# Alignment paths to experts: tests and row normalisation on another engine, statistics by quarters, part of the logits behind the first expert

## The chip, the cores and the metric

The kernel runs on one core of a Trainium2 chip. Its engines are TensorE (PE, with its weight load PEld), VectorE (DVE), ScalarE (ACT), GpSimd (POOL) and SyncE (SP), which issues the DMAs. Each has its own instruction stream, and they wait for one another by semaphores. The metric is the device time of one execution in microseconds. PE's granted clock is given as a share of 2.4 GHz: 1.00 is 2.4 GHz and 0.50 is 1.2 GHz.

## The reference

32 sequences of 128 tokens with 128 features, f32. Four blocks follow one another, each added to x with a tanh gate:

```python
x = x + tanh(g_xattn[0]) * mlstm_attention(layernorm(x), ctx, ctx, ...)
x = x + tanh(g_ffn[0])   * quantised_ffn(layernorm(x), W1, b1, W2, b2)
x = x + tanh(g_xattn[1]) * aligned(ctx, layernorm(x))
x = x + tanh(g_ffn[1])   * experts(layernorm(x), gate_weight, w1, b1, w2, b2)

def align_one(small, large):                # 128 tokens each
    R = dtw_cost(pairwise_euclidean(small, large))
    i_idx, j_idx, valid = backtrack(R)       # the cheapest monotone path
    return zeros.at[j_idx].add(small[i_idx] * valid)

def experts(x, ...):                         # 8 experts, hidden size 512
    logits = einsum('bld,ed->ble', x, gate_weight)
    kth_val = sort(logits.reshape(-1))[4 * 128 * 6 - 1]
    gates = logits * (logits >= kth_val)
    h = gelu(einsum('bld,ehd->bleh', x, w1) + b1)
    y = einsum('bleh,edh->blde', h, w2) + b2.T
    return einsum('blde,ble->bld', y, gates)
```

The part in question lies between the third block's backtracking and the fourth block's first experts.

## The kernel before

The residual `xs` stays in SBUF, tokens on partitions, 32 sequences side by side; they are worked in eight groups of four (`G4` = 8), a group being a tile of 128x512. The order on each engine is written out by hand, and every hand-over is a semaphore that counts up.

Backtracking leaves for each row of the path where it enters and leaves it. From these DVE makes a centre `ec` and a half width `eT[:, 1]` for each sequence (up to line 1106). Then, by groups:

- ACT makes the distances `pathm[:, b] = |iota2 + ec|`, 128x128 for each sequence (line 621, semaphore `far_ready`).
- DVE compares them with the half width and so writes the 0/1 matrix of the path, `path` (`path_of`, a `tensor_scalar` through the helper at line 676, `path_ready`).
- PE multiplies it with the context, `bank(1 + g % 2)` (line 1501, `expanded`).
- DVE adds the product to `xs` (`add_expanded`, line 1116) and takes `bn_stats` of each sequence (`stats`, line 1122).
- Layer norm goes by halves of 16 sequences: `ln_stats` makes mean and variance in seven small operations (lines 682 to 688), ACT takes the root (line 426), `ln_scales` the reciprocal (line 700), and `ln_apply` normalises 16 sequences, one instruction each, into `x4` (line 676 again, `ln_done`). Groups 0 to 3 are normalised when DVE has all but the last group's sum; then come the last add, its statistics, and the second half.
- PE transposes a group (line 1510, banks 6 and 7) and, one group behind, makes its logits in f32 with `x4f` as weights and eight columns as moving data (line 1516, bank 3). ACT copies the transposed bank twice: f32 into one of two slots of `x4f` (line 631) and bf16 into `x4h` (line 632). POOL subtracts: `x4l = x4f - x4h` (line 397).
- After the last logits PE waits for all of `x4l` and starts the experts.

For each block of 512 tokens (8) and each expert (8) PE makes the hidden part with three bf16 products for each of four banks (`hidden`, lines 1525 to 1527), ACT applies GELU (line 639), POOL in blocks 0 and 1 and DVE later split off the low half, and PE makes the outputs from 48 small products (`outputs`, lines 1541 to 1543). `outputs` of an expert follows `hidden` of the next. Blocks 0 and 1 are computed before the gates are known: meanwhile DVE looks for the threshold in 17 rounds, each of which compares all logits with candidates and lets PE sum the counts over partitions with a product with ones (`counts`, line 1549, put into `hidden` of expert n for round n; PE waits there for `count_ready`). In block 2 the gates' products with the bias go between the experts in nine steps (`gated_bias`, lines 1555 and 1559): step e transposes gates of group e - 1 and multiplies those of group e - 2, with an ACT copy between them and one behind. From line 1190 on DVE makes the low halves and the gated sums.

Of the kernel before, what the change touches and what calls it, by code (L numbers as in the profile page):

```python
# [15 lines left out]
P = 128  # L16
B = 32
# [38 lines left out]
def program(nc, x, ctx_, g_x, g_f, if_w, if_b, on_w, a_w1, a_b1, a_w2, a_b2, gate_w, m_w1, m_b1, m_w2, m_b2, out):  # L56
    with ExitStack() as stack:
# [3 lines left out]
        def sem(name):  # L61
# [64 lines left out]
        x4f = A[:, 8192:9216].rearrange("p (s t) -> p s t", s=2)  # L126
# [95 lines left out]
            "x4_turned", "x4_kept", "x4_split", "logits_done", "count_ready", "count_all", "gates_ready", "late_added", "bias_added", "gb_kept",  # L222
# [87 lines left out]
        def _(pool):  # L310
# [83 lines left out]
            for g in range(G4):  # L394
                pool.wait_ge(S["x4_kept"], g + 1)
                w = slice(512 * g, 512 * g + 512)
                pool.tensor_tensor(x4l[:, w], x4f[:, g % 2, :], x4h[:, w], ALU.subtract).then_inc(S["x4_split"], 1)  # L397
# [12 lines left out]
        def _(act):  # L410
# [208 lines left out]
            for g in range(G4):  # L619
# [3 lines left out]
            ln(3, (0,))  # L623
            for g in range(G4):
                if g == 3:
                    ln(3, (1,))
# [25 lines left out]
            for e in range(1, E + 2):  # L652
                if e < E:
                    gelu(NS, e)
                if e - 1 < G4:
                    act.wait_ge(S["gt_turned"], e)
                    act.activation(gtT[:, (e - 1) % 2, :], PS[0:32, 6, 0:P], ACT.Copy).then_inc(S["gt_kept"], 1)
                if e >= 2:
                    act.wait_ge(S["gb_done"], e - 1)
                    act.activation(gbias[:, 512 * (e - 2):512 * (e - 1)], bank(7), ACT.Copy).then_inc(S["gb_kept"], 1)  # L660
# [6 lines left out]
        def _(dve):  # L667
# [10 lines left out]
            def ln_stats(n, h):  # L678
                w = slice(16 * h, 16 * h + 16)
# [428 lines left out]
            def path_of(g):  # L1108
                dve.wait_ge(S["far_ready"], g + 1)
                for b in range(4 * g, 4 * g + 4):  # L1110
                    ins = ts(path[:, b, :], pathm[:, b, :], eT[:, 1, b:b + 1], None, ALU.is_le)
                ins.then_inc(S["path_ready"], 1)

# [31 lines left out]
            link(dve.tensor_copy(lgf, bank(3, 0, B * E)))  # L1145
# [104 lines left out]
        def _(pe):  # L1250
# [244 lines left out]
            for g in range(G4):  # L1495
# [6 lines left out]
                ins.then_inc(S["expanded"], 1)  # L1502
            pe.wait_ge(S["w_split"], 2 * E)
            for g in range(G4 + 1):
                if g < G4:
# [110 lines left out]
```

## Time and profile before

| | us |
|---|---|
| median of 3 runs (lowest, highest) | 780.08 (777.25, 780.39) |
| the profiled execution's own time | 777.89 |
| its span | 776.2 |
| busy: PE / DVE / ACT / POOL | 597.0 / 582.3 / 399.8 / 125.9 |
| mean granted clock of PE | 0.881 |
| first distances on ACT | 374.67 |
| first transpose of x4's second half | 406.40 |
| first product of the experts | 418.32 |
| first output product of the experts | 425.49 |

Times of the trace count from the start of the span. A row of the timeline or of a group gives an instruction's full duration, which can overlap its successor's; the chain of waits gives only what each piece adds to it. An L and a number is a line of the kernel; line 676 is a helper for every `tensor_scalar` of DVE, so those are told apart by their tiles.

### The profile page before, as it was taken

The page shows a single profiled execution, that of the slowest core. Times are in us where ns is not written, and L with a number is a line of the kernel's source. Part 1 is how long each engine was busy: PE and PEld are TensorE (multiplying, and loading weights), DVE is VectorE, ACT ScalarE, POOL GpSimd, SP SyncE. Part 2 cuts the span into 40 slices and gives each one's busy share as a digit, 9 for nine tenths or more (in the row PEclk, how much of TensorE's full clock was granted, in tenths as well). Part 3 has the DMA queues.
Part 4 walks back from the last instruction along what each step waited for, and adds up shares of the span by engine and source line. Part 5 has one row for each costly group of instructions (what it writes and reads, how often), then busy time and mean ns, then how long its engine had stood idle before and what let it go on. Part 6 is the DMA issues. An engine that isn't in the chain of part 4 may idle for free.

```text
span 776.2 us, 17215 instructions
## 1 busy us (share of the span) xinstructions
PE 597.0 (77%) x6431; PEld 430.5 (55%) x6499; DVE 582.3 (75%) x1736; ACT 399.8 (52%) x719; POOL 125.9 (16%) x158
## 2 busy tenths in 40 slices
PE   3975899843505870038469999999999999999997
PEld 3973344321204570027357777766577777777776
DVE  6657688898978819999794565566587788887775
ACT  1434778677826342238425556555444544554552
POOL 3000044434000000000025777700000000000000
PEclk9999999975557795559766999999999999999999
DMA  8000000000001000005000000000000000010000
GB/s 227 29 0 1 3 2 4 2 1 0 0 0 55 1 3 0 1 14 149 1 0 1 2 2 1 2 2 1 1 16 2 15 0 14 0 41 0 14 2 14
DMA packets 19548, 12.09 MB, mean 16 GB/s; under 512 B 1085, under 2 KB 18329, under 8 KB 19481
## 3 DMA queue, kind: packets, MB, share of 16 engines
q1 hardware_dynamic: 19480, 11.22, 5.3%
q8 instruction: 40, 0.66, 0.3%
q14 instruction: 28, 0.22, 0.1%
HBM read 9.12 MB, written 2.10 MB: 14 GB/s over the span
## 4 chain that ended last, share of the span: by engine, by line
PE 64%; DVE 28%; ACT 3%; issue 3%; SPq 1%; DMA 0%; another core or an unknown queue 0%; DVEq 0%
PE PS L1526 8%; PE PS L1541 7%; PE PS L1543 7%; PE PS L1542 7%; PE PS L1527 7%; PE PS L1525 5%; DVE A L1094 3%; PE PS L1274 3%; DVE Bm L1065 3%; PE PS L1348 3%; DVE hmm L986 2%; DVE hmm L987 2%; DVE Bm L676 2%; PE PS L1358 2%; PE PS L1454 1%
## 5 line engine op out<-in xcount | busy, mean ns | idle before, releaser
L639 ACT ACTIVATE A<-PS,small_t 128x512 f32<-128x512 f32 x256 | 168.3, 687 | 124.0 <-PE PS L1527 122.4
L1541 PE MATMUL PS<-kT_w,A 128*128 128x128 bf16 x1024 | 174.8, 219 | 0.0
L1543 PE MATMUL PS<-kT_w,A 128*128 128x128 bf16 x1024 | 174.8, 219 | 0.0
L1542 PE MATMUL PS<-kT_w,A 128*128 128x128 bf16 x1024 | 174.8, 219 | 0.0
L1190 DVE TENSOR_TENSOR A<-A 128x512 bf16<-128x512 f32 x192 | 123.6, 688 | 11.9 <-ACT A L639 10.5
L1541 PEld LDWEIGHTS PS<-kT_w,A 128*128 128x128 bf16 x1024 | 100.2, 98 | 11.3 <-issue 4.6
L1542 PEld LDWEIGHTS PS<-kT_w,A 128*128 128x128 bf16 x1024 | 100.2, 98 | 6.6
L1526 PE MATMUL PS<-A,xn_w 128*128 128x512 bf16 (+1 forms) x256 | 98.1, 383 | 3.6 <-issue 0.4
L1543 PEld LDWEIGHTS PS<-kT_w,A 128*128 128x128 bf16 x1024 | 100.2, 98 | 0.0
L1527 PE MATMUL PS<-A,xn_w 128*128 128x512 bf16 (+1 forms) x256 | 98.3, 384 | 0.0
L1198 DVE SCALAR_TENSOR_TENSOR xs<-PS,A,xs 128x128 f32 (+1 forms) x192 | 54.1, 344 | 55.9 <-PE PS L1543 55.9
L1525 PE MATMUL PS<-A,xn_w 128*128 128x512 bf16 (+1 forms) x193 | 74.2, 385 | 0.0
L401 POOL TENSOR_TENSOR A<-A 128x512 bf16<-128x512 f32 x64 | 64.5, 1041 | 22.4 <-ACT A L639 22.4
L1527 PEld LDWEIGHTS PS<-A,xn_w 128*128 128x128 bf16 x256 | 25.2, 99 | 31.1 <-issue 1.6
L1462 PE MATMUL PS<-identf,Bm 64*64 64x64 f32 x2 | 0.6, 298 | 51.7 <-DVE Bm L1065 51.7
L1525 PEld LDWEIGHTS PS<-A,xn_w 128*128 128x128 bf16 x256 | 26.9, 105 | 22.2 <-issue 1.9
L1526 PEld LDWEIGHTS PS<-A,xn_w 128*128 128x128 bf16 x256 | 25.3, 99 | 21.6 <-issue 1.4
L397 POOL TENSOR_TENSOR A<-A 128x512 bf16<-128x512 f32 x8 | 9.4, 1184 | 158.8 <-ACT A L632 158.8
L1462 PEld LDWEIGHTS PS<-identf,Bm 64*64 64x64 f32 x2 | 0.3, 127 | 52.0 <-issue 49.2
L1348 PE MATMUL PS<-A,kT_w 32*128 32x256 f32 x256 | 25.2, 435 | 3.8 <-DVE A L862 3.8
L643 ACT ACTIVATE Bm<-PS 128x512 f32 x16 | 9.6, 597 | 33.3 <-PE PS L1543 33.3
L862 DVE TENSOR_TENSOR A<-Bm,PS 128x512 f32<-128x512 f32 x32 | 20.6, 684 | 7.5 <-ACT Bm L473 4.8
(317 smaller groups left out, 1203.8 us busy)
## 6 DMA issues: line engine op xcount, KB each, us to landing
slab<-in_L_ffn_w_dram SPq DMA_DIRECT2D x16, 256.0 KB, 3.0
xs<-in_x_dram SPq DMA_DIRECT2D x4, 512.0 KB, 5.7
cs<-in_ctx_dram SPq DMA_DIRECT2D x4, 512.0 KB, 6.5
out_dram<-xs SPq DMA_DIRECT2D x8, 256.0 KB, 2.5
xn_w<-in_L_ffn_W_dram SPq DMA_DIRECT2D x2, 256.0 KB, 2.8
onw_b<-n_L_xattn_outnorm_w_dram SPq DMA_DIRECT2D x1, 64.0 KB
ab_b<-in_L_ffn_b_dram SPq DMA_DIRECT2D x1, 64.0 KB
b2blk<-in_L_ffn_b_dram SPq DMA_DIRECT2D x4, 4.0 KB
```

The source lines that it names most:

```text
L401: pool.tensor_tensor(hl[:, e % 2, c, :], hf[:, e % 2, c, :], hh[:, e % 2, c, :], ALU.subtract).then_inc(S["h_low_pool"], 1)
L639: act.activation(hf[:, e % 2, c, :], bank(c), ACT.Gelu_apprx_tanh, bias=b1).then_inc(S["h_gelu"], 1)
L1065: dve.tensor_tensor_scan(rt[:, s + 1, 1:RTW], mins[:, s], dd[:, s], rt[:, s + 1, 0:1], ALU.min, ALU.add).then_inc(S["row_done"], 1)
L1190: dve.tensor_tensor(hl[:, e % 2, c, :], hf[:, e % 2, c, :], hh[:, e % 2, c, :], ALU.subtract).then_inc(S["h_low_dve"], 1)
L1198: ins = dve.scalar_tensor_tensor(out=row, in0=bank(4 + e % 2, P * k, P * k + P), scalar=gate, in1=row, op0=ALU.mult, op1=ALU.add)
L1348: ins = pe.matmul(PS[:, 2 + r, 0:256], kT[rows, P * b:P * b + P], qTm[rows, :, P * b:P * b + P], start=True, stop=True)
L1525: pe.matmul(bank(c), w1h[:, e, c, :], x4h[:, xw], start=True, stop=False)
L1526: pe.matmul(bank(c), w1h[:, e, c, :], x4l[:, xw], start=False, stop=False)
L1527: pe.matmul(bank(c), w1l[:, e, c, :], x4h[:, xw], start=False, stop=True).then_inc(S["h_ready"], 1)
L1541: pe.matmul(o, hh[:, e % 2, c, t], w2h[:, e, c, :], start=(c == 0 and k == 0), stop=False, skip_group_check=True)
L1542: pe.matmul(o, hh[:, e % 2, c, t], w2l[:, e, c, :], start=False, stop=False, skip_group_check=True)
L1543: ins = pe.matmul(o, hl[:, e % 2, c, t], w2h[:, e, c, :], start=False, stop=(c == NC - 1), skip_group_check=True)
```

## The change

- `path_of` moves from DVE to POOL, for all eight groups.
- The normalisation of groups 0 to 5 moves from DVE to POOL (`x4_apply`, semaphore `x4_early`); groups 6 and 7 stay on DVE (`x4_late`). POOL's order is: tests 0 to 4, rows 0 and 1, tests 5 and 6, rows 2 and 3, test 7, rows 4 and 5.
- Statistics become variances by quarters of eight sequences (four calls of `ln_stats` with `each=8`), with a root on ACT (`x4_root`) and a reciprocal on DVE (`x4_scale`, `x4_scales`) for each.
- `x4l` is made by DVE from the transposed bank in PSUM (`x4_low`) in place of POOL from `x4f`. The bank is free for the transpose two groups later only after it. `x4f` becomes eight slots in another place, the copy order on ACT is turned (bf16 first), and the logits go to bank 5.
- PE's order: expansions 0 to 3; then transposes in pairs with expansions 4 to 7 and logits 0 to 3 between them; transposes 6 and 7; hidden products of the first expert; logits 4 to 7; the other experts. The first expert waits for one `x4l` and the last sum alone.
- Round n of the count is summed in `hidden` of expert n + 1, and the nine steps of the gated bias begin at expert 2 of block 2, not at expert 1; three of them then have no `hidden` of block 2 beside them, where it was two.

```diff
@@ gpsimd
-            for g in range(G4):
-                pool.wait_ge(S["x4_kept"], g + 1)
-                w = slice(512 * g, 512 * g + 512)
-                pool.tensor_tensor(x4l[:, w], x4f[:, g % 2, :], x4h[:, w], ALU.subtract).then_inc(S["x4_split"], 1)
+            def path_of(g):
+                pool.wait_ge(S["far_ready"], g + 1)
+                for b in range(4 * g, 4 * g + 4):
+                    ins = pool.tensor_scalar(path[:, b, :], pathm[:, b, :], eT[:, 1, b:b + 1], None, ALU.is_le)
+                ins.then_inc(S["path_ready"], 1)
+            def x4_apply(g):
+                pool.wait_ge(S["x4_scales"], g // 2 + 1)
+                for b in range(4 * g, 4 * g + 4):
+                    ins = pool.tensor_scalar(x4[:, b, :], xs[:, b, :], lnt[:, 3, b:b + 1], lnt[:, 7, b:b + 1], ALU.subtract, ALU.mult)
+                ins.then_inc(S["x4_early"], 1)
+            for g in range(5):
+                path_of(g)
+            for g in range(2):
+                x4_apply(g)
+            for g in range(5, 7):
+                path_of(g)
+            for g in range(2, 4):
+                x4_apply(g)
+            path_of(G4 - 1)
+            for g in range(4, 6):
+                x4_apply(g)
@@ scalar
+            def x4_root(j):
+                w = slice(8 * j, 8 * j + 8)
+                act.wait_ge(S["bn_done"], 7 + j)
+                act.activation(lnt[:, 5, w], lnt[:, 4, w], ACT.Sqrt, bias=cst[:, 0:1]).then_inc(S["ln_sqrt"], 1)
+            def x4_keep(g):
                 act.wait_ge(S["x4_turned"], g + 1)
-                if g >= 2:
-                    act.wait_ge(S["logits_done"], g - 1)
-                    act.wait_ge(S["x4_split"], g - 1)
-                act.activation(x4f[:, g % 2, :], bank(6 + g % 2), ACT.Copy)
                 act.activation(x4h[:, 512 * g:512 * g + 512], bank(6 + g % 2), ACT.Copy).then_inc(S["x4_kept"], 1)
+                act.activation(x4f[:, g], bank(6 + g % 2), ACT.Copy).then_inc(S["x4_kept"], 1)
+            for g in range(6):
+                far(g)
+            x4_root(0)
+            for g in range(6, G4):
+                far(g)
+            for j in range(4):
+                if j >= 1:
+                    x4_root(j)
+                x4_keep(2 * j)
+                x4_keep(2 * j + 1)
@@ vector
+            def x4_scale(j):
+                dve.wait_ge(S["ln_sqrt"], 7 + j)
+                dve.reciprocal(lnt[:, 7, 8 * j:8 * j + 8], lnt[:, 5, 8 * j:8 * j + 8]).then_inc(S["x4_scales"], 1)
+            def x4_low(g):
+                w = slice(512 * g, 512 * g + 512)
+                dve.wait_ge(S["x4_kept"], 2 * g + 2)
+                dve.tensor_tensor(x4l[:, w], bank(6 + g % 2), x4h[:, w], ALU.subtract).then_inc(S["x4_split"], 1)
             for g in range(G4):
-                path_of(g)
-                if g >= 1:
-                    add_expanded(g - 1)
-                if g >= 2:
-                    ins = stats(g - 2)
-                if g == 5:
-                    link(ins)
-                    ln_stats(3, 0)
-                if g == 6:
-                    ln_scales(3, 0)
-            ln_apply(0, xs, x4)
-            add_expanded(7)
-            stats(6)
-            link(stats(7))
-            ln_stats(3, 1)
-            ln_scales(3, 1)
-            ln_apply(1, xs, x4)
+                add_expanded(g)
+                if g % 2 == 0 and g >= 2:
+                    x4_scale(g // 2 - 1)
+                ins = stats(g)
+                if g % 2:
+                    link(ins)
+                    ln_stats(3, g // 2, 8)
+                if g in (4, 6):
+                    for k in (g - 4, g - 3):
+                        x4_low(k)
+            x4_scale(3)
+            for g in range(G4 - 2, G4):
+                (four rows of tensor_scalar into x4, then x4_late)
+            for g in range(4, G4):
+                x4_low(g)
@@ tensor
+            def turn_x4(g):
+                (waits for x4_early or x4_late)
+                if g >= 2:
+                    pe.wait_ge(S["x4_kept"], 2 * g - 2)
+                    pe.wait_ge(S["x4_split"], g - 1)
+                (four transposes into bank 6 + g % 2)
+            for g in range(4):
+                expand(g)
+            for j in range(3):
+                turn_x4(2 * j)
+                turn_x4(2 * j + 1)
+                if j < 2:
+                    expand(2 * j + 4)
+                    expand(2 * j + 5)
+                if j >= 1:
+                    logits(2 * j - 2)
+                    logits(2 * j - 1)
+            turn_x4(6)
+            turn_x4(7)
+            pe.wait_ge(S["expanded_added"], G4)
+            pe.wait_ge(S["x4_split"], 1)
...
-                    if isinstance(blk, int) and blk * E + e < ROUNDS and c == (1 if blk or e else 2):
-                        counts(blk * E + e)
+                    if isinstance(blk, int) and 1 <= blk * E + e <= ROUNDS and c == 1:
+                        counts(blk * E + e - 1)
...
             hidden(0, 0)
+            for g in range(4, G4):
+                logits(g)
+            pe.wait_ge(S["x4_split"], G4)
...
-            for e in range(1, E + 2):
+            for e in range(1, E + 3):
                 if e < E:
                     hidden(NS, e)
-                if e == 1:
+                if e == 2:
                     pe.wait_ge(S["gates_ready"], 1)
                     pe.wait_ge(S["b2_in"], 64)
-                gated_bias(e)
+                if e >= 2:
+                    gated_bias(e - 1)
```

## Rows read from the trace of the kernel before

**Rows 1.** The page's slices of the span, 19.4 us each: busy tenths of TensorE and of VectorE

```profile
PE   3975899843505870038469999999999999999997
DVE  6657688898978819999794565566587788887775
```

**Rows 2.** The chain of waits, 374 to 407 us: start us, us, what

```profile
374.67 1.28 ACT Bm L621 x4
...
379.77 0.78 DVE Bm L676 x4
380.55 0.66 DVE xs L1116
381.21 0.78 DVE bns L1122 x4
...
388.66 0.19 DVE lnt L682
...
389.57 0.17 DVE lnt L688
...
394.47 5.92 DVE A L676 x16
...
406.40 1.12 PE PS L1510 x4
```

**Rows 3.** Windows by stage: us, busy of PE, PEld, DVE, ACT, POOL, clock, DMA, GB/s

```profile
374.67:394.40 19.73, 11.46 (x62) 10.22 (x63) 16.95 (x72) 9.76 (x33) 0.00 (x0) 0.76 0.00 1
394.40:406.40 12.00, 7.47 (x45) 6.54 (x44) 11.45 (x39) 4.43 (x9) 4.69 (x4) 0.64 0.00 1
406.40:418.32 11.92, 11.69 (x56) 11.65 (x58) 4.13 (x13) 4.34 (x8) 4.74 (x4) 0.50 0.00 1
418.32:425.49 7.17, 6.74 (x27) 2.94 (x27) 4.06 (x22) 5.30 (x8) 3.97 (x4) 0.83 0.00 0
```

**Rows 4.** Groups, 374 to 421 us: busy us, mean ns | idle us before, releaser

```profile
L621 ACT ACTIVATE Bm<-iota,ec 128x128 f32<-128x128 f32 x32 | 9.5, 389 | 8.3 <-DVE ec L676 8.3
...
L632 ACT ACTIVATE A<-PS 128x512 bf16<-128x512 f32 x8 | 4.8, 594 | 0.0
...
L676 DVE TENSOR_SCALAR Bm<-Bm,eT 128x128 f32<-128x128 f32 x32 | 6.9, 280 | 1.7 <-ACT Bm L621 1.6
```

**Rows 5.** Timeline of TensorE: start us, us, what, count, idle before and releaser

```profile
387.25 1.16 PE L1501 MATMUL PS<-cs,Bm 128*128 128x128 f32 x8 [1.05 <-DVE Bm L676]
...
390.59 2.07 PE L1501 MATMUL PS<-cs,Bm 128*128 128x128 f32 x8 [2.18 <-DVE Bm L676]
...
397.90 0.97 PEld L1516 LDWEIGHTS PS<-small_t,A 128*128 128x128 f32 x8 [0.76 <-ACT A L632]
...
406.40 1.12 PE L1510 MATMUL PS<-identf,A 128*128 128x128 f32 x4 [3.32 <-DVE A L676]
...
407.31 1.72 PE L1516 MATMUL PS<-small_t,A 128*128 128x8 f32 x8
```

**Rows 6.** Groups of GpSimd, whole span; the last line is line 397's own view

```profile
L338 POOL TENSOR_SCALAR identn<-identb 128x128 bf16<-128x128 bf16 x1 | 0.3, 297 | 0.1
...
L372 POOL TENSOR_TENSOR A<-Bm,onw_b 128x128 f32<-128x128 f32 x4 | 1.7, 453 | 0.1
...
L397 POOL TENSOR_TENSOR A<-A x8: 1151/1154/1282, 397.9 to 416.1; 128x512 bf16<-128x512 f32 x8
```

**Rows 7.** The timeline, TensorE's second count among the experts

```profile
423.96 0.39 PE L1549 MATMUL PS<-sel,ones 128*128 128x3 f32 x2 [0.43 <-DVE A L1156]
```

**Rows 8.** The timeline, TensorE's last step of the gated bias

```profile
555.89 1.12 PE L1559 MATMUL PS<-b2blk,A 32*128 32x512 f32 x2 [0.69 <-ACT Bm L660]
```

**Rows 9.** Windows of two to six us

```profile
382.00:388.00 6.00, 3.07 (x22) 2.69 (x23) 6.00 (x25) 2.13 (x8) 0.00 (x0) 1.00 0.01 3
...
390.00:392.00 2.00, 1.41 (x6) 1.41 (x7) 2.00 (x9) 0.09 (x1) 0.00 (x0) 0.52 0.00 0
...
400.00:402.00 2.00, 1.79 (x11) 1.70 (x10) 2.00 (x8) 0.57 (x2) 1.47 (x2) 0.58 0.00 0
```

More of the change, by code:

```diff
@@ L125, in program @@
         x4l = A[:, 6144:8192].bitcast(BF16)
-        x4f = A[:, 8192:9216].rearrange("p (s t) -> p s t", s=2)
+        x4f = Bm[:, 8192:12288].rearrange("p (g t) -> p g t", g=G4)
         hf = A[:, 9216:13312].rearrange("p (s c t) -> p s c t", s=2, c=NC)
@@ L618, in _, with far @@
             act.wait_ge(S["e_kept"], 1)
-            for g in range(G4):
+            def far(g):
                 for b in range(4 * g, 4 * g + 4):
@@ L651, in _ @@
                 keep_y(blk, E - 1)
-            for e in range(1, E + 2):
+            for e in range(1, E + 3):
                 if e < E:
                     gelu(NS, e)
[L655 to L660, printed above, removed]
+                if 2 <= e < G4 + 2:
+                    act.wait_ge(S["gt_turned"], e - 1)
+                    act.activation(gtT[:, (e - 2) % 2, :], PS[0:32, 6, 0:P], ACT.Copy).then_inc(S["gt_kept"], 1)
+                if e >= 3:
+                    act.wait_ge(S["gb_done"], e - 2)
+                    act.activation(gbias[:, 512 * (e - 3):512 * (e - 2)], bank(7), ACT.Copy).then_inc(S["gb_kept"], 1)
             with act.Fori(NS + 1, G4) as blk:
@@ L676, in ts, with ln_stats @@
                 return dve.tensor_scalar(out, a, s1, s2, op0, op1)
-            def ln_stats(n, h):
-                w = slice(16 * h, 16 * h + 16)
+            def ln_stats(n, h, each=16):
+                w = slice(each * h, each * h + each)
                 t = lambda k: lnt[:, k, w]
@@ L1106, in _ @@
             ts(ec[:], ec[:], pm[:, 11:12], pm[:, 12:13], ALU.mult, ALU.add).then_inc(S["e_kept"], 1)
[L1108 to L1112, printed above, removed]
             def add_expanded(g):
@@ L1494, in _, with expand @@
             pe.matmul(PS[HALF:P, 3, 0:2 * B], flip, logs[:, :, 1], start=True, stop=True).then_inc(S["e_turned"], 1)
-            for g in range(G4):
+            def expand(g):
                 pe.wait_ge(S["path_ready"], g + 1)
@@ L1502, in _, with logits @@
                 ins.then_inc(S["expanded"], 1)
-            pe.wait_ge(S["w_split"], 2 * E)
-            for g in range(G4 + 1):
-                if g < G4:
-                    pe.wait_ge(S["ln_done"], 3 * G4 - 4 + g + 1)
-                    if g >= 2:
-                        pe.wait_ge(S["x4_kept"], g - 1)
-                    for k in range(4):
-                        ins = pe.transpose(bank(6 + g % 2, P * k, P * k + P), x4[:, 4 * g + k, :], identf[:])
-                    ins.then_inc(S["x4_turned"], 1)
-                if g >= 1:
-                    pe.wait_ge(S["x4_kept"], g)
-                    for k in range(4):
-                        b = 4 * (g - 1) + k
-                        ins = pe.matmul(bank(3, E * b, E * b + E), x4f[:, (g - 1) % 2, P * k:P * k + P], small_t[:, 84:92], start=True, stop=True)
-                    ins.then_inc(S["logits_done"], 1)
-            pe.wait_ge(S["x4_split"], G4)
+            def turn_x4(g):
+                if g < 6:
+                    pe.wait_ge(S["x4_early"], g + 1)
+                else:
+                    pe.wait_ge(S["x4_late"], g - 5)
+                if g >= 2:
+                    pe.wait_ge(S["x4_kept"], 2 * g - 2)
+                    pe.wait_ge(S["x4_split"], g - 1)
+                for k in range(4):
+                    ins = pe.transpose(bank(6 + g % 2, P * k, P * k + P), x4[:, 4 * g + k, :], identf[:])
+                ins.then_inc(S["x4_turned"], 1)
+            def logits(g):
+                pe.wait_ge(S["x4_kept"], 2 * g + 2)
+                for k in range(4):
+                    b = 4 * g + k
+                    ins = pe.matmul(bank(5, E * b, E * b + E), x4f[:, g, P * k:P * k + P], small_t[:, 84:92], start=True, stop=True)
+                ins.then_inc(S["logits_done"], 1)
+            pe.wait_ge(S["w_split"], 2 * E)
+            for g in range(4):
[13 more added lines that the diff above has]
+            pe.wait_ge(S["x4_split"], 1)
             def hidden(blk, e):
@@ L1567, in _ @@
                 outputs(blk, E - 1)
-            for e in range(1, E + 2):
+            for e in range(1, E + 3):
                 if e < E:
                     hidden(NS, e)
-                if e == 1:
+                if e == 2:
                     pe.wait_ge(S["gates_ready"], 1)
                     pe.wait_ge(S["b2_in"], 64)
-                gated_bias(e)
+                if e >= 2:
+                    gated_bias(e - 1)
                 if e < E:
```

12 lines of the change are left out of this document (6 added, 6 removed).

## The prediction

> **What bounds the kernel now.** I read the page first, then the chain of waits, then windows by stage, then groups of instructions. The page's slices show TensorE (PE) full from the twenty-second slice on, behind a stretch in which VectorE (DVE) is the full engine [rows 1]. The chain goes through DVE from 374.67 us, where ScalarE (ACT) begins the distances |2k - c|, to the last normalised quarter, and from 406.40 through PE alone [rows 2]. By windows: 374.67 to 406.40 is DVE's (16.95 of 19.73 us, then 11.45 of 12.00), 406.40 to 418.32 PE's (11.69 of 11.92) at a granted clock of 0.50, the 1.2 GHz level [rows 3]. From 418.32 the experts begin, PE-bound to the end, so what counts is when the first output product starts, 425.49 now: every microsecond of it is a microsecond of the end, except what the later part of the diff adds. GpSimd (POOL) does nothing from 374.67 to 394.40 [rows 3].
>
> **The pieces and their prices.** Rows of groups and of the timeline overlap their successors, so for runs of like instructions I use what each adds, start to start. By the chain [rows 2] four path tests cost 0.78 us on DVE, one add of the expanded group 0.66, four statistics 0.78, the small operations from statistics to variance 1.08 (388.66 to 389.74), a row of the normalisation 0.37 (5.92 for 16). There are thirty-two tests [rows 4] and as many statistics. ACT makes a group of distances in 1.16 (32 starts in 9.46) and copies a bank of 512 in 0.594, 0.50 from start to start [rows 4]. On PE an expansion of a group is 1.16 us at 2.4 GHz and 2.07 at 1.2 GHz, a group's transpose 1.12 at 1.2 GHz, the logits of a group 1.72 at 1.2 GHz and, by their weight loads, 0.97 at 2.4 GHz [rows 5]. Some 0.2 of each is the last product's way out (the chain has 1.51 for the logits of 1.72), which the next work on PE doesn't wait for and the consumer does.
>
> **Part 1: tests and rows on POOL.** 32 tests (6.2 us by start to start) and 24 of the 32 row normalisations (24 x 0.37 = 8.9 us) leave DVE: 15.1 us. In exchange DVE gets the eight low parts x4l, read straight from PSUM, where POOL read the f32 copy: 8 x 0.66 (the add, of the same width and also with one PSUM operand, is the nearest row) = 5.3. Four variances of quarters instead of two of halves add 2 x 1.08. DVE falls by 7.6 us. POOL's price per instruction is not in the trace: no POOL tensor_scalar with a column operand over 128 f32 stands there. Low bound: the two-operation form with constants on 128 bf16 took 0.297, with the next start 0.24 later; high bound: the two-input tensor_tensor of 128 f32, 0.453 [rows 6]; but column operands could be worse than either, so for the range I go up to 0.6, a third above the highest row. I take 0.28 for a test and 0.35 for a row, near the one-input row with something for the columns. The eight late rows stay on DVE.
>
> **Part 2: the chain in the new order.** Times with the PE clock between its levels: an expansion 1.40 (between 0.95 and 1.85 without the way out), a transpose 0.65 (0.45 to 0.85), logits 1.35; 0.1 to 0.3 for each hand-over.
> First distances 375.95; four tests on POOL, 377.1; expansion, 379.0; DVE adds and takes statistics of groups 0 and 1, then the variance, 382.95. ACT's root is hidden under the add of group 2; the reciprocal ends at 383.8. POOL normalises groups 0 and 1 (8 x 0.35): 386.8. Transpose 1, 387.6. Behind it on PE stands expansion 4: 389.0. DVE adds group 4, reciprocal 1: 390.2. POOL, groups 2 and 3: 393.2; transpose 3, 394.0; expansion 6, queued behind that transpose: 395.4. DVE: add 6, reciprocal 2, statistics 6, low parts 2 and 3, add 7, statistics 7, variance (0.66 + 0.22 + 0.78 + 1.32 + 0.66 + 0.78 + 1.08): 401.2. The last root waits on ACT behind the four copies of groups 4 and 5, which wait for POOL (396.7 to 399.5) and transpose 5: root 402.7, reciprocal 403.1. Eight late rows 2.96: 406.0. Then a wait that before doesn't have: a bank is free for transpose 6 only when DVE has made low part 4, which is queued behind the late rows: 406.7; transpose 6, low part 5, transpose 7: **408.2** for the first expert product, where 418.32 stands now: 10.1 us earlier.
>
> **Part 3: what is given back.** The logits of groups 4 to 7 aren't removed; they stand on PE between the first expert's hidden products and the next's. Four groups cost 3.9 us at 2.4 GHz, 6.9 at 1.2 GHz; 5.4 is taken. The shift of the counting by one expert takes away the 0.43 us for which PE waited for the second count [rows 7]: the first count now has a whole first product around it. The 7.17 us from first expert product to first output product become 7.17 - 0.43 + 5.4, and 0.5 (between 0 and 1.3) if the clock has fallen in the narrow logits and the next six products go at 1.2 GHz as the first six do now. That is 12.6: output products from 420.8 instead of 425.49, 4.7 us gained.
>
> **Part 4: the gated bias, one expert later.** Of its nine steps two now stand with no hidden product between them, afterwards three. A lone step goes at 1.12 + 0.69 = 1.81 us (PE waits for ACT's copy) [rows 8], of which 1.05 is PE work that is only moved: 0.8 lost. Nothing to 1.8 is possible. Gates come later by one expert in DVE's order too, but its next low parts are wanted only one hidden product later.
>
> **Sum.** -10.1 + 5.4 (12.6 against 7.17) + 0.8 = -3.9 us. ACT's table load of 1.28 us before the first GELU has the logits beside it now. The copies of x4f into eight slots instead of two remove waits and cost nothing: ACT is busy for 9.76 + 4.43 of 31.7 us here [rows 3]. SP's queue has no edit. The profiled execution took 777.89 us (span 776.2, 1.7 around it) and would be 774.0; the runs' median is 780.08 (777.25 to 780.39), 2.2 above the profiled one, and by that the same sum gives **776.2**.
>
> **A rule weighed.** The trace shows POOL at 1.28 us at most for the subtraction of 512 when DVE runs beside it and 1.15 at least [rows 6]: no lock is to be seen there. The Trainium skill (GPSIMD Engine Reference, 3. Performance versus the Vector engine) holds VectorE about twice as fast for elementwise work, though it lets one-input operations off (4.1 Engine selection). Twice DVE's own 0.195 and 0.37 on POOL would be 0.39 and 0.74, and the chain above then ends at 417.3 with a total of +5.2 us, 785.3. The one-input row at 0.24 us start to start speaks against it. I count this in the slow-POOL rival.
>
> **The clock, the uncertain middle.** The granted clock was 1.00 from 382 to 388 with PE busy half the time, fell about 390, in an idle stretch of 2.18 us [rows 5], and was 0.50 even for the full stretch of transposes and logits from 406.40; in the experts' first 7.17 us it averaged 0.83, so 2.4 us of them went at 1.2 GHz [rows 3]. From 400 to 402, in the narrow logits, it fell to 0.58 [rows 9]. So logits alone don't lift it, and gaps end it. The new order has POOL's pace in front of PE, and gaps of 2 to 3 us before transposes 0 and 6.
>
> **Rivals.**
> Warm PE: if the expansions, spread out through the stage, hold the clock at 1.00, the chain ends at 405.3, logits take 3.9 and the first six products save 1.3: 405.3 + 9.3 + 0.8 - 425.49 = -10.1, so 770.0. For it: 382 to 388. Against it: the fall at 390. Chance 0.2.
> Cold PE: 1.2 GHz throughout: chain 412.1, logits 6.9, next six products +1.3: +2.3, so 782.4. The pipeline then gives nothing, since PE's own stretch of 11.9 us is only moved. Chance 0.15.
> Slow POOL, the one that ends slower: 56 instructions in series before groups 4 and 5 are ready. At 0.6 us for each they alone are 33.6 us; the chain ends at 418.6, total +6.5: 786.6. It decides from 0.475 us per instruction on (chain end 412.1 = 425.49 - 13.4). For it: column operands and a comparison are forms that no row has. Against it: both one-input rows under 0.3. Chance 0.15.
> My forecast has 0.5, its own range 773 to 780.
>
> **Range and chances.** Between the warm and the cold case, and a little of the slow one: 770 to 783. The measurement can't tell less than about 0.5%, 3.9 us, from no change, and the forecast lies on that line: half of its 0.5 counts as faster. With the warm case: faster 0.46; same (the other half, most of the cold one): 0.38; slower 0.16.
>
> **What would show it.** In the profile after: the first expert product near 408 (405 to 412); POOL tests at 0.25 to 0.3 us start to start and rows at 0.3 to 0.4; 64 narrow logits products, half of them behind the first expert; first output product near 421; the wait of transpose 6 put down to DVE's low part; three lone bias steps at the end of block 2. The forecast is wrong if POOL's pace is over 0.47 us, if the granted clock is above 0.8 or at 0.5 in all of 377 to 408, or if the experts' own rhythm changes, for which I see no reason.

## The result and the profile after

The changed kernel is slower, by about 1%: 787.34 us in the median (785.8 to 788.22, 4 runs) against 780.24 (777.25 to 781.0, 4 runs) for the kernel before on the same chip, ratio 1.0096 (95% interval 1.0065 to 1.0127). The forecast was 776.2 within 770 to 783.

The page of the kernel after, against [rows 1] (busy by engine, then the slices):

```profile
PE 603.5 (77%) x6499; PEld 431.5 (55%) x6499; DVE 573.0 (73%) x1704; ACT 400.6 (51%) x721; POOL 154.2 (20%) x206
...
DVE  6657678898979719998543556676478788887775
...
POOL 3000045434000000000893777700000000000000
```

DVE is no longer the full engine ahead of the experts: in the three slices that hold this stretch (the 20th to the 22nd) it read 794 and now reads 543, and POOL, 025 before (its subtractions, then work for the first experts), reads 893. The two groups of POOL that the change made (busy us, mean ns | idle before, releaser; [rows 4] has the tests as DVE's):

```profile
L403 POOL TENSOR_SCALAR A<-xs,lnt 128x128 f32<-128x128 f32 x24 | 18.8, 795 | 1.6 <-DVE lnt L1151 1.6
L397 POOL TENSOR_SCALAR Bm<-Bm,eT 128x128 f32<-128x128 f32 x32 | 18.6, 601 | 126.3 <-ACT Bm L640 126.3
```

The chain of waits after, where [rows 2] had DVE from 374.67 to 406.40 (start us, us, what):

```profile
374.82 1.28 ACT Bm L640 x4
...
376.21 11.63 POOL Bm L397 x20
387.84 6.26 POOL A L403 x8
394.10 4.64 POOL Bm L397 x8
398.74 6.26 POOL A L403 x8
405.00 2.33 POOL Bm L397 x4
407.33 1.50 issue
408.89 0.07 POOL A L403
...
409.68 5.47 POOL A L403 x7
415.19 1.13 PE PS L1547 x4
416.34 0.60 ACT A L650
...
417.43 0.20 ACT lnt L646
...
417.89 2.14 DVE A L706 x8
420.03 0.61 DVE A L1156
...
420.78 1.94 PE PS L1547 x8
422.72 0.43 PE PS L1578
```

From 376.21 to 415.15 the chain is POOL's own row of instructions, with one gap, from 407.33 to 408.89, in which it waits for the third reciprocal (the group's idle 1.6 us behind DVE's L1151). Twenty tests take 11.63 us, 0.58 each; eight rows 6.26, 0.78 each. The end of the chain is as forecast: the last root behind ACT's copies, eight late rows on DVE, low part 4, transposes 6 and 7. The windows by stage, as [rows 3]:

```profile
374.82:394.40 19.58, 9.63 (x37) 8.09 (x38) 8.88 (x35) 10.84 (x35) 18.19 (x29) 0.59 0.00 1
394.40:406.40 12.00, 6.35 (x31) 5.76 (x30) 5.54 (x20) 2.55 (x6) 12.00 (x19) 0.64 0.00 0
406.40:422.72 16.32, 11.55 (x64) 10.88 (x64) 8.90 (x31) 4.26 (x10) 7.18 (x10) 0.60 0.00 1
422.72:432.90 10.18, 10.18 (x61) 6.40 (x60) 3.57 (x15) 6.89 (x11) 5.48 (x6) 0.89 0.00 0
```

DVE is busy for 8.88 of 19.58 us where it was full, POOL for 18.19 of 19.58 and 12.00 of 12.00. First expert product at 422.7 (418.3 before), first output product at 432.7 (425.5), and from there 351.3 us to the end of the span (350.7).

One caution for all profiles below. In the attention stage, which no kernel here edits, the same instructions started up to 3.5 us apart from profile to profile (the last scores at 160.3 us in one, 163.8 in another), so I compare stages from the first distances on, which the cores reach at 374.7 to 378.1:

| kernel | first distances to first expert product: forecast by prices / measured | first distances to end of span | ratio to before (95% interval) |
|---|---|---|---|
| before | - / 43.6 | 401.5 | 1 |
| after | 33.5 in the prediction / 47.9 | 409.3 | 1.0096 (1.0065 to 1.0127) |
| tests back on DVE | 46.1 / 45.9 | 406.3 | 1.0074 (1.0053 to 1.0096) |
| rows back on DVE | 39.6 / 38.9 | 399.7 | 0.9985 (0.9966 to 1.0003) |
| both on DVE | 40.4 / 40.1 | 401.4 | 1.0021 (1.0007 to 1.0034) |
| rows as wide products on POOL | 42.8 / 41.6 | 403.2 | 1.0018 (1.0001 to 1.0034) |
| as rows back on DVE, logits in front | 44.6 / 44.3 | 405.2 | 1.0048 (1.0032 to 1.0064) |
| rows on ACT, low parts on POOL | 33 / 34.0 | 395.7 | 0.9924 (0.9907 to 0.9942) |
| rows on ACT, low parts on DVE | 35.7 / 35.9 | 401.1 | 0.9982 (0.9968 to 0.9995) |
| rows on ACT, low parts on POOL, late rows on DVE | 33 / 33.7 | 396.1 | 0.9925 (0.9901 to 0.9949) |
| before, subtraction behind the rows | 41.3 / 41.3 | 398.8 | 0.9969 (0.9956 to 0.9981) |

The first column is good to some 0.3 us: a few records of PE are missing, the very first product of the experts among them in the kernel before and in the three runs with tests, rows or both back on DVE, and the chain has a product 0.2 us later than the timeline.

The second column has a spread of its own. Behind the last steps of the gated bias in block 2 TensorE's granted clock can fall to 0.50, for a length that differs from profile to profile, also where the instructions there are the same. Windows of 25 us around these steps (columns as in [rows 3]) of the kernel before, of "before, subtraction behind the rows" and of "logits in front":

```profile
550.00:575.00 25.00, 24.00 (x236) 15.91 (x239) 15.31 (x34) 11.03 (x19) 0.00 (x0) 0.93 0.04 12
550.00:575.00 25.00, 24.31 (x247) 16.16 (x247) 16.86 (x42) 12.30 (x21) 0.00 (x0) 1.00 0.04 12
552.00:577.00 25.00, 23.84 (x213) 14.53 (x211) 13.45 (x31) 10.57 (x18) 0.00 (x0) 0.86 0.04 12
```

From the first output product to the end of the span these three take 350.7, 348.9 and 352.8 us. So a difference of some 2 us in the second column, and 4 between the last two of these, can come from there; the ratios rest on the medians of all runs, and how often each length occurs in those is not known.

### The profile page after: what moved, and what is told of

Same layout as the page of the kernel before. It is cut to its first block, busy times and chain, and to the rows that moved or that the text cites. A ratio compares the mean times of both kernels' runs of the same rounds, so it can differ in the third digit from the quotient of the medians.

```text
span 784.1 us, 17295 instructions
## 1 busy us (share of the span) xinstructions
PE 603.5 (77%) x6499; PEld 431.5 (55%) x6499; DVE 573.0 (73%) x1704; ACT 400.6 (51%) x721; POOL 154.2 (20%) x206
## 4 chain that ended last, share of the span: by engine, by line
PE 64%; DVE 25%; POOL 5%; ACT 3%; issue 2%; SPq 1%; DMA 0%; DVEq 0%; POOLq 0%
PE PS L1594 7%; PE PS L1596 7%; PE PS L1595 7%; PE PS L1578 7%; PE PS L1579 7%; PE PS L1580 7%; DVE A L1124 3%; PE PS L1308 3%; PE PS L1382 3%; DVE Bm L1095 3%; POOL Bm L397 2%; POOL A L403 2%; DVE hmm L1016 2%; DVE hmm L1017 2%; PE PS L1392 2%
## 5 line engine op out<-in xcount | busy, mean ns | idle before, releaser
L1594 PE MATMUL PS<-kT_w,A 128*128 128x128 bf16 x1024 | 174.8, 219 | 0.0
L1594 PEld LDWEIGHTS PS<-kT_w,A 128*128 128x128 bf16 x1024 | 100.2, 98 | 10.6 <-issue 3.8
L1579 PE MATMUL PS<-A,xn_w 128*128 128x512 bf16 (+1 forms) x256 | 98.3, 384 | 0.0
L1578 PE MATMUL PS<-A,xn_w 128*128 128x512 bf16 (+1 forms) x256 | 98.1, 383 | 0.0
L1580 PE MATMUL PS<-A,xn_w 128*128 128x512 bf16 (+1 forms) x256 | 98.1, 383 | 0.0
L420 POOL TENSOR_TENSOR A<-A 128x512 bf16<-128x512 f32 x64 | 64.6, 1041 | 31.6 <-ACT A L669 31.6
L397 POOL TENSOR_SCALAR Bm<-Bm,eT 128x128 f32<-128x128 f32 x32 | 18.6, 601 | 126.3 <-ACT Bm L640 126.3
L1208 DVE TENSOR_SCALAR_CACHE_REDUCE sel<-PS 128x3 f32<-128x3 f32 (+1 forms) x16 | 2.6, 161 | 33.3 <-PE PS L1602 33.3
```

Of the source, the lines that this page charges most:

```text
L397: ins = pool.tensor_scalar(path[:, b, :], pathm[:, b, :], eT[:, 1, b:b + 1], None, ALU.is_le)
L420: pool.tensor_tensor(hl[:, e % 2, c, :], hf[:, e % 2, c, :], hh[:, e % 2, c, :], ALU.subtract).then_inc(S["h_low_pool"], 1)
L1578: pe.matmul(bank(c), w1h[:, e, c, :], x4h[:, xw], start=True, stop=False)
L1579: pe.matmul(bank(c), w1h[:, e, c, :], x4l[:, xw], start=False, stop=False)
L1580: pe.matmul(bank(c), w1l[:, e, c, :], x4h[:, xw], start=False, stop=True).then_inc(S["h_ready"], 1)
L1594: pe.matmul(o, hh[:, e % 2, c, t], w2h[:, e, c, :], start=(c == 0 and k == 0), stop=False, skip_group_check=True)
```

## The experiments

**What an instruction costs on POOL.** A kernel that only times instructions on loaded tiles (one execution).

```diff
+ for k in range(8):
+     pool.tensor_scalar(py[:, k, :], xs[:, k, :], 0.5, None, ALU.is_le)    # and: a column; mult; two operations
...
+ for k in range(4):
+     pool.tensor_tensor(four tiles of py, four of xs, four columns with a step of zero, ALU.subtract)
```

> This kernel computes nothing of the reference: it only times instructions of GpSimd and VectorE on loaded x, eight or sixteen of each form in a row. Three readings of GpSimd's 0.58 us for a path test and 0.78 us for a normalised row of 128 f32. (A) The operand that is a column of one value per partition costs: the forms with constants stay at 0.24 to 0.30 us start to start, with one column 0.58, with two 0.78, and a column form over 512 elements costs about 0.3 us more than one over 128, since the columns are paid once. (B) The comparison and the second operation cost, by element: constant forms are as slow as column forms, and 512 elements take nearly four times as long as 128. (C) VectorE, which worked beside it, slowed GpSimd: alone, all forms are at 0.30 or less. Second question: the rows of the normalisation on VectorE took 0.26 us alone but 1.25 us whenever GpSimd's 512-wide subtraction ran in the kernel before. If the two lock each other out, VectorE's 24 rows beside GpSimd's eight subtractions of 512 show some of 1.2 us and beside GpSimd's column rows some of 0.9 to 1.0 us; if it was chance, all are at 0.23 to 0.26 us. Statistics (bn_stats, one input) should show no such thing.

The timeline of POOL in that kernel: start us, us of the whole run, line, forms, count. Lines 51 to 66 are, in order: is_le with a constant, is_le with a column, mult with each, subtract and mult with constants, the same with columns; 69 and 72 the two column forms over 512; 75 a two-input subtraction of 512 whose second input is four columns, spread by a step of zero (78, not shown, multiplies in the same way); 83 a subtraction of two tiles of 512, and 88 and 103 rows with two columns, all three beside work of DVE.

```profile
10.69 3.98 POOL L51 TENSOR_SCALAR py<-xs 128x128 f32<-128x128 f32 x8 [10.27 <-DMA xs<-in_x_dram]
14.78 4.64 POOL L54 TENSOR_SCALAR py<-xs,col 128x128 f32<-128x128 f32 x8
19.50 3.99 POOL L57 TENSOR_SCALAR py<-xs 128x128 f32<-128x128 f32 x8
23.59 4.66 POOL L60 TENSOR_SCALAR py<-xs,col 128x128 f32<-128x128 f32 x8
28.34 4.91 POOL L63 TENSOR_SCALAR py<-xs 128x128 f32<-128x128 f32 x8
33.36 6.21 POOL L66 TENSOR_SCALAR py<-xs,col 128x128 f32<-128x128 f32 x8
39.67 6.17 POOL L69 TENSOR_SCALAR py<-xs,col 128x512 f32<-128x512 f32 x4
45.95 8.24 POOL L72 TENSOR_SCALAR py<-xs,col 128x512 f32<-128x512 f32 x4
54.27 4.03 POOL L75 TENSOR_TENSOR py<-xs,col 128x512 f32<-128x512 f32 x4
...
66.93 9.80 POOL L83 TENSOR_TENSOR py<-xs 128x512 f32<-128x512 f32 x8 [4.52 <-DVEq L123]
81.11 12.96 POOL L88 TENSOR_SCALAR py<-xs,col 128x128 f32<-128x128 f32 x16 [4.37 <-DVEq L128]
...
116.83 4.23 POOL L103 TENSOR_SCALAR py<-xs,col 128x128 f32<-128x128 f32 x4 [0.21 <-DVEq L143]
```

Start to start: 0.498 and 0.580 for one operation with a constant and a column, comparison and product alike; 0.614 and 0.776 for two operations. Over 512 elements 1.54 and 2.06. So neither reading (A) nor (B) holds whole: of 0.58 only 0.08 is the column, and of 0.78 0.16; a comparison costs no more than a product. Most of it goes by element: (1.54 - 0.58) / 384 is 2.5 ns, and 3.3 ns with two operations. (C) falls: alone they are as slow as in the kernel. The two-input tensor_tensor of 512 takes 1.01, less than two thirds of the tensor_scalar of 512 with one column. DVE's side of the same kernel:

```profile
62.60 4.19 DVE L121 TENSOR_SCALAR dy<-xs,col 128x128 f32<-128x128 f32 x16 [61.74 <-POOLq L80]
66.94 13.97 DVE L125 TENSOR_SCALAR dy<-xs,col 128x128 f32<-128x128 f32 x24
81.09 8.82 DVE L130 TENSOR_SCALAR dy<-xs,col 128x128 f32<-128x128 f32 x32 [0.18 <-DVE dy L125]
94.24 6.29 DVE L135 BATCH_NORM_STATS2 bst<-xs 128x6 f32<-128x128 f32 x32 [4.33 <-POOLq L90]
...
116.80 3.60 DVE L145 TENSOR_TENSOR dy<-xs 128x128 f32<-128x128 f32 x16 [3.22 <-POOLq L100]
```

Sixteen rows alone are 0.26 each. Beside POOL's subtractions eight were done in 9.76 us, 1.22 for each pair of one row and one subtraction. That is near the sum of 0.26 for a row and 1.01 for a two-input form of 512, as if each ran only while the other didn't; this is called the lock below. Beside POOL's column rows 32 take 8.82, 0.28 each, and statistics 0.20 as alone. Beside DVE's two-input additions POOL's rows rise from 0.78 to 1.06.

**Tests, rows, or both back on DVE.**

```diff
# tests (first run), rows (second), both (third): the same instructions, on DVE
-                    ins = pool.tensor_scalar(path[:, b, :], pathm[:, b, :], eT[:, 1, b:b + 1], None, ALU.is_le)
+                    ins = ts(path[:, b, :], pathm[:, b, :], eT[:, 1, b:b + 1], None, ALU.is_le)
...
-                    ins = pool.tensor_scalar(x4[:, b, :], xs[:, b, :], lnt[:, 3, b:b + 1], lnt[:, 7, b:b + 1], ALU.subtract, ALU.mult)
+                    ins = ts(x4[:, b, :], xs[:, b, :], lnt[:, 3, b:b + 1], lnt[:, 7, b:b + 1], ALU.subtract, ALU.mult)
```

> The changed kernel with the path tests back on VectorE; rows of groups 0 to 5 stay on GpSimd. Theory P (GpSimd's price per instruction, 0.58 and 0.78 us in series, is the whole loss, the new order costs next to nothing): GpSimd has 24 x 0.78 = 18.8 us left; but the rows of a pair can only start when its reciprocal is there, so the first expert product comes at about 420.9 instead of 422.7, and the time is about 785.5 us (ratio to before 1.007). Theory C (the new couplings are the loss: transposes wait for the low parts, expansions stand behind transposes, PE at 1.2 GHz in the gaps; GpSimd only fills waits): 787, no change.

> The changed kernel with the row normalisation of groups 0 to 5 back on VectorE (0.26 us a row), tests stay on GpSimd. Theory P: GpSimd 32 x 0.58 = 18.6 us from 376.2, it is through at 394.9; VectorE gets 24 x 0.26 = 6.2 us; first expert product at about 414.4, time about 779 us (ratio 0.998). Theory C: the order is the same, so at least 785 us.

> The changed kernel with tests and rows on VectorE, GpSimd does nothing in this stretch; pipeline, quarters, low parts on VectorE, logits behind the first expert and the later bias stay. Theory P: VectorE is the bound again (27 us of its own), first expert product at about 415.2, time about 779.8 us (ratio 1.000), so the pipeline without GpSimd is worth nothing, and nothing is lost. Theory C: at least 785 us, as the couplings are all there.

Measured: 785.43, 777.79 and 780.68 us, before 778.78; ratios in the table. Theory P hits all three within 2 us and each stage within 0.7 us (table). Theory C wanted 787 for the first, whose runs reach from 782.46 to 787.36, and 785 or more for the other two, none of whose runs exceeds 781.82: it falls by these two. The rows are what makes the change slow. With them back the pipeline is level with the kernel before (0.9985, its interval reaches 1.0003); with the tests back too it is 0.2% behind.

**Rows on POOL in the cheaper form.**

```diff
-                for b in range(4 * g, 4 * g + 4):
-                    ins = pool.tensor_scalar(x4[:, b, :], xs[:, b, :], lnt[:, 3, b:b + 1], lnt[:, 7, b:b + 1], ALU.subtract, ALU.mult)
+                link(pool.tensor_tensor(g4(x4, g), g4(xs, g), last(lnt[:, 3, 4 * g:4 * g + 4], P), ALU.subtract))
+                pool.tensor_tensor(g4(x4, g), g4(x4, g), last(lnt[:, 7, 4 * g:4 * g + 4], P), ALU.mult).then_inc(S["x4_early"], 1)
```

> The changed kernel with one edit: a group's rows on GpSimd as two tensor_tensor instructions of 512 with the columns spread by a step of zero, in place of four tensor_scalar of 128 with two columns. Alone the forms took 1.01 us for each 512 and 0.776 for each 128, so a group is 2.1 us instead of 3.1. Theory P (GpSimd's price in series is the loss): first expert product 42.8 us after the first distances (47.9 in the changed kernel), time about 782 us, ratio to before 1.004. If the price beside VectorE is not what it is alone, the group stays at 2.5 us or more and the time at 784 or more.

780.59 us, before 779.69, ratio 1.0018: of the 7 us lost most came back by one edit of POOL's instruction form. A subtraction and a product of 512, 1.04 us each, stand in the place of four rows, 3.1 us. The group of the subtractions:

```profile
L402 POOL TENSOR_TENSOR A<-xs,lnt 128x512 f32<-128x512 f32 x6 | 6.3, 1042 | 1.6 <-DVE lnt L1150 1.6
```

**The logits in front again.**

```diff
+            logits(4)
+            logits(5)
             turn_x4(6)
             turn_x4(7)
+            logits(6)
+            logits(7)
...
             hidden(0, 0)
-            for g in range(4, G4):
-                logits(g)
```

> The run with the rows on VectorE and the tests on GpSimd, with the logits of groups 4 to 7 put back ahead of the first expert (4 and 5 before the transposes of 6 and 7, 6 and 7 behind them). What is this part of the change worth? By the prices of the trace: the first expert product comes 5 us later, but then 3.3 us fewer stand before the first output product: 2 us slower than that run, so about 779.8 us, ratio 1.001. Rival: the logits only fill gaps in which PE waits for VectorE, so it is as fast as that run (777.8), and the split of the logits is worth nothing.

782.02 us, 4 us more than with the logits behind the first expert, where 2 were expected. The rival falls. The first expert product came 5.4 us later (5 expected), but the way from there to the first output product was only 1.4 us shorter (8.1 against 9.5) in place of 3.3: the expert's first products ran at 1.2 GHz for some 5.5 us (0.43 us each until 424.7, in the chain). Narrow logits had run right ahead of them; that these are the cause is what the trace suggests, not something that I isolated.

**Each piece where it is cheapest.**

```diff
# DVE: tests; a column -m*r after each reciprocal.  ACT: all rows
+                link(dve.reciprocal(lnt[:, 7, w], lnt[:, 5, w]))
+                dve.scalar_tensor_tensor(out=lnt[:, 6, w], in0=lnt[:, 3, w], scalar=-1.0, in1=lnt[:, 7, w], op0=ALU.mult, op1=ALU.mult)
...
+                    ins = act.activation(x4[:, b, :], xs[:, b, :], ACT.Identity, scale=lnt[:, 7, b:b + 1], bias=lnt[:, 6, b:b + 1])
# POOL: low parts (left out in the second version, where DVE keeps them)
+                pool.tensor_tensor(x4l[:, w], x4f[:, g, :], x4h[:, w], ALU.subtract).then_inc(S["x4_split"], 1)
# PE: expand(4), expand(5) ahead of turn_x4(0); no wait for x4_split where POOL has the low parts
```

> Each piece of the pipeline on the engine where its measured price is lowest: tests on VectorE (0.195 us), all 32 rows on ScalarE as x*r + (-m*r) with two columns (0.3 us each by its distances, which carry one column), low parts by GpSimd as one subtraction of 512 (1.0 to 1.2 us) from the eight slots of x4f, expansions 4 and 5 ahead of the first transposes. Theory P (only the price of column instructions on GpSimd made the change slower, the pipeline itself is sound): first expert product 33 us after the first distances (before 43.65, changed kernel 47.9), time about 771.7 us, ratio 0.991. Theory C (the finer order brings as many new waits as it removes): 777 or more. GpSimd's subtractions may lock VectorE's last tests and cost 1 to 2 us.

> As the run with the low parts on GpSimd, but these stay on VectorE from PSUM, and a transpose waits for them as in the changed kernel. Theory P: VectorE is the bound again with 27 us; first expert product 35.7 us after the first distances, time about 774.5 us, ratio 0.9945. Theory C: 778 or more.

The first is the fastest version: 773.14 us, 0.9924, where 771.7 and 0.991 were expected; theory C's 777 or more falls. The second comes at 777.28 us, 0.9982, where 774.5 and 0.9945 were expected: a miss, just under theory C's 778. The pieces of the first, busy us and mean ns:

```profile
L649 ACT ACTIVATE A<-xs,lnt 128x128 f32<-128x128 f32 x32 | 12.7, 492 | 0.0
...
L409 POOL TENSOR_TENSOR A<-Bm,A 128x512 bf16<-128x512 f32 x8 | 9.2, 1159 | 152.2 <-ACT Bm L644 152.1
...
L723 DVE TENSOR_SCALAR Bm<-Bm,eT 128x128 f32<-128x128 f32 x32 | 6.8, 279 | 1.9 <-ACT Bm L633 1.9
```

ACT is its bound now, at 3.07 us for eight rows in the chain (0.38 each; 0.3 was expected). The second has its first expert product where it was forecast, but 13.9 us pass from there to the first output product, where the first needs 10.3. The chains of both, second kernel first; L1594 and L1589 are the sixteen logits products of groups 4 to 7 (32 records):

```profile
415.93 4.30 PE PS L1594 x32
420.23 0.44 PE PS L1625
```

```profile
413.93 3.47 PE PS L1589 x32
417.40 0.23 PE PS L1620
```

In the second kernel the clock falls within the logits (0.78 over their 4.30 us) and the next expert's products take 0.43 in place of 0.22 us each. The 3.6 us between 13.9 and 10.3 are more than the 2.8 by which the second version misses its forecast. What decides between the two was not isolated. An edit on top of the first version:

```diff
-            x4_apply(6)          # ACT
-            x4_apply(7)
+            (eight rows of groups 6 and 7 by ts on DVE, behind x4_scale(3))
```

> The fastest version so far (tests on VectorE, rows on ScalarE, low parts on GpSimd) with the rows of groups 6 and 7 on VectorE, which is idle by then, since ScalarE now ends the stretch with 3.07 us for eight rows (0.38 each). VectorE's eight take 2.1 us, unless one of GpSimd's subtractions runs beside them: each would cost 0.9 more. Expected by the prices: first expert product 0.6 to 1.3 us earlier than in that version (34.0 us after the first distances there), time about 772.2 us, ratio 0.9915. Rival: the lock takes it back, no difference from 0.9924.

773.56 us, 0.9925: no difference. The lock was there. The timeline has two of GpSimd's subtractions beside the eight rows, which take 3.96 us in place of 2.1, the longest 1282 ns:

```profile
406.52 3.96 DVE L721 TENSOR_SCALAR A<-xs,lnt 128x128 f32<-128x128 f32 x8
...
407.08 2.30 POOL L409 TENSOR_TENSOR A<-Bm,A 128x512 bf16<-128x512 f32 x2 [2.92 <-ACT Bm L644]
```

But it is not what took the gain back. PE has the logits of groups 2 and 3 (3.21 us, at a granted clock of 0.50) ahead of transpose 6 in its order; they end at 410.24, and the transposes follow without a wait. So the rival's lock is seen and its number is right, but the wait that ends last is PE's own. In the profile the first expert product comes 0.3 us earlier than in the version without the edit and the first output product 1.2 us earlier (43.2 against 44.4 us after the first distances); the clock in block 2, low for longer there (0.86 over 25 us against 0.93), takes this back.

**The lock in the kernel before.**

```diff
             for g in range(G4):
+                pool.wait_ge(S["ln_done"], 3 * G4 + 4)
                 pool.wait_ge(S["x4_kept"], g + 1)
...
-                pool.tensor_tensor(x4l[:, w], x4f[:, g % 2, :], x4h[:, w], ALU.subtract).then_inc(S["x4_split"], 1)
+                pool.tensor_tensor(x4l[:, w], x4f[:, g, :], x4h[:, w], ALU.subtract).then_inc(S["x4_split"], 1)
```

> The kernel before with one edit: GpSimd's subtractions of 512 begin only when VectorE's last normalised row is done (x4f has eight slots for it). Theory L (the two engines lock each other out: VectorE's row takes 1.2 us beside a subtraction and 0.26 alone): all 32 rows at 0.26, the first transpose of the second half comes 2.7 us earlier, first expert product about 2.3 us earlier since GpSimd needs 9.2 us after the rows; time about 776.4 us, ratio 0.997. Theory N (no lock; the long rows have another cause): rows as before, and the first expert product some 3 us later, as GpSimd starts late: 782 us.

776.02 us, ratio 0.9969, as theory L has it. ACT's copies into eight slots also wait no longer for the logits and the subtraction of two groups before; this part of the edit is not separated from POOL's wait. The line's own view there (duration min/median/max, first and last start):

```profile
L674 DVE TENSOR_SCALAR A<-xs,lnt x32: 329/339/345, 395.2 to 407.2; 128x128 f32<-128x128 f32 x32
...
L398 POOL TENSOR_TENSOR A<-Bm,A x8: 1152/1154/1157, 407.6 to 415.4; 128x512 bf16<-128x512 f32 x8
```

No row is above 345 ns any more. The same view of the kernel before:

```profile
L676 DVE TENSOR_SCALAR A<-xs,lnt x32: 330/342/1262, 394.4 to 410.0; 128x128 f32<-128x128 f32 x32
```

There the longest took 1262 ns. So the lock is what made rows long, and theory N falls. How much the wait is worth is less clear than the hit on 776.4 suggests. The first expert product comes 2.3 us earlier after the first distances, as forecast. The first output product comes only 1.0 us earlier (49.8 against 50.8): all nine wide products before the first count go at 1.2 GHz in the chain (0.43 us each), where before the last two had 0.22. The other 1.8 us by which this profile's stretch to the end is shorter are in the clock, which didn't fall in block 2. That the profile ends as forecast is in part luck.

## Why the prediction was wrong

**POOL's price (part 1) is the step that failed.** It took 0.28 us for a test and 0.35 for a row; they are 0.58 and 0.78, 37.3 us for 56 instructions instead of 17.4. With these two numbers put into the prediction's own chain, and 0.26 for the late rows, its groups 2 and 3 are normalised at 404.7; as there, rows 4 and 5 can start 3.5 us later, behind expansion 6 and the third reciprocal, and take 6.2; the rest of its chain is 7.8 us. The first expert product then comes at about 422.2; it came at 422.7. So the slow-POOL rival, given 0.15, is what happened, and its turning point of 0.475 us per instruction was passed: the mean is 0.67 (37.3 / 56). Where exactly the turn lies no run shows. The bounds were wrong, too. [Rows 6] gave 0.297 from a bf16 tile with constants and called it the nearest row; in f32 two operations with constants take 0.61, so its closeness was in the name of the instruction and not in its data type (how much of the difference the data type makes was not timed). "Both one-input rows under 0.3" is this one row of [rows 6]. The trace of before did have GpSimd's tensor_scalar in f32 with two operations, unused by the prediction: line 357, seven times 128x32 at 216 ns, nearly three quarters of the bf16 row's 297 for a quarter of its elements. And the two-input 0.453 was taken as the dearest form, while at 512 elements the two-input form is the cheaper one (1.01 against 1.54 us). The widened end, 0.6, rested on no row, and the normalising rows lie beyond even that.

**The rule that was weighed.** Twice DVE's price, 0.39 and 0.74 with a total of 785.3, was set aside for the closeness of that one row. Measured, POOL's 0.58 and 0.78 are three times DVE's 0.195 and 0.26, and the runs' median is 787.34. The exemption of one-input operations, which the prediction named with it (Trainium skill, GPSIMD Engine Reference, 4.1 Engine selection), is what these rows contradict: even with one operation and a constant GpSimd's f32 instruction takes 0.498 us.

**The lock that was missed.** "No lock is to be seen there" was read from POOL's durations, 1.15 to 1.28 us; the one that waits is DVE. It stood in the trace of before. Windows of DVE's rows there, without and with a subtraction beside them:

```profile
394.39:396.00 1.61, 1.61 (x7) 0.50 0.00 0
...
397.93:400.40 2.47, 2.47 (x3) 0.99 0.00 0
```

Seven rows in 1.61 us (0.23 each), then three in 2.47 (0.82; subtractions are busy for 2.38 of the 2.47). The 0.37 us of the prediction was a mean of 0.26 and 1.2. The Trainium skill (SBUF — State Buffer, Who interferes with whom) says that a tensor_scalar of VectorE in a two-port mode and GpSimd hold a shared pair of ports in turn, each for a whole instruction; beside the subtractions the traces agree, with 1.22 us for a pair in the timing kernel; which mode VectorE was in, none of them shows. Beside POOL's tensor_scalar the measurement differs: VectorE's rows stay at 0.28. Had this been read, DVE's 8.9 us for 24 rows would have been 6.2, and the alternative, to move the subtraction and not the rows, would have been in sight. No run moves the subtraction alone; to delay it has the ratio 0.9969, and the best version, 0.9924, combines the tests and rows taken off POOL, the rows put on ACT and the subtraction kept on POOL.

**The other numbers.** From first expert to first output product: 12.6 forecast, 10.0 measured, as the clock held its 2.4 GHz through the logits (3.47 us for four groups) and nothing was lost in the next expert; with the low parts on DVE and the rows on ACT it is 13.9. The gated bias: 0.8 forecast, 0.6 as the longer way from the first output product to the end (351.3 against 350.7). That it is so near is not proof: the same way differs by 1.5 us between profiles of kernels with the same bias order (351.3, and 352.8 with the logits in front), by the clock's fall at these steps. The second count's wait went, as said. Transpose 6 waits for low part 4 (chain, 420.03 to 420.78), as said. The warm and the cold PE rivals did not come into play: the clock was 0.59 to 0.64, between its levels, as the forecast had it, but POOL's pace hid it. "Gaps end it" is too narrow: in the second version with the rows on ACT the clock fell within the logits, with PE busy for all of their 4.30 us.

**The sum as it came.** First expert product 4.4 later in place of 10.1 earlier, 2.8 more to the first output product (5.4), 0.6 on the way to the end (0.8 of bias): 7.9 us of span.

## What to carry to other kernels

Before work is moved to an engine, find a row of that engine with the same operation, data type, operand kind and width; if there is none, the price is unknown and not near the closest name, and it should be timed by itself. Where one engine's like instructions show a mean well above their minimum, look at what its neighbour runs at that time before taking the mean as a price: such a mean hid 1.2 us rows among those of 0.26 here, and a wait that kept the two engines apart came with a gain (ratio 0.9969). Move a piece to the engine that has both slack and a cheap form of it: here ACT took the rows at 0.38 us each. By itself that brought the pipeline with all on DVE from 1.0021 to 0.9982 (with another order of expansions and tests); only together with the low parts on POOL was it 0.9924.

## What was not expected of the hardware

On GpSimd in f32 a tensor_scalar of 512 elements (1.54 us with one column, 2.06 with two) is dearer than a two-input tensor_tensor of 512 (1.01 us, the second input a spread column). VectorE's row and GpSimd's 512-wide subtraction shut each other out, GpSimd's 128-wide tensor_scalar does not (rows at 0.28 us beside it). And TensorE's clock can fall within sixteen narrow products or hold through them: 4.30 against 3.47 us for the same logits, and 2.3 us more for the twelve wide products of the next expert (5.2 against 2.9). It can also fall or hold behind the same bias steps: 350.7 and 348.9 us from the first output product to the end.
